# GpSimd makes the scaled and clamped scores of VectorE's exponential

## What is computed

```python
def wl_step(acc, wl):
    cpm, iw = wl                       # cos(phase_modulators) of 16 heads, one weight
    m = cpm[None, :, None, None]
    scores = jnp.einsum('bhqd,bhkd->bhqk', Q * m, K * m) * SCALE
    scores = scores * jnp.cos(KERR * scores * scores)
    attn = jax.nn.softmax(scores, axis=-1)
    out = jnp.einsum('bhqk,bhkd->bhqd', attn, V)
    return (acc + out * iw, None)
```

## Time and profile before

| | us |
|---|---|
| median of 3 runs (6973.81 to 6976.5) | 6975.69 |
| the profiled execution | 6975.18 |
| its span, first to last instruction | 6973.7 |
| ScalarE busy in the span | 6796.0 |
| TensorE busy in the span | 6097.9 |
| VectorE busy in the span | 6061.4 |
| GpSimd busy in the span | 148.7 |

### The profile page before, as it was taken

How to read it: one execution, slowest core, us unless ns; L and a number is a source line. 1 busy time by engine, 2 the same in 40 slices (tenths; PEclk the granted TensorE clock), 3 DMA queues, 4 the chain that set the end, 5 groups by cost and what they waited for, 6 DMA issues and landing times.

```text
span 6973.7 us, 125248 instructions
## 1 busy us (share of the span) xinstructions
PE 6097.9 (87%) x47364; PEld 2296.8 (33%) x47364; DVE 6061.4 (87%) x8039; ACT 6796.0 (97%) x1209; POOL 148.7 (2%) x244
## 2 busy tenths in 40 slices
PE   7888888888889888889888898888888888988888
PEld 3222222222333333333333333333333333333336
DVE  7998899899888888898888888888988888888884
ACT  6999999999999999999999999999999999999993
POOL 0000000000000000000000000000000000000000
PEclk8999999999999999999999999999999999999999
DMA  2000000000101001000010010010010100100100
GB/s 60 3 5 5 5 3 5 5 3 5 33 22 30 18 28 30 17 28 27 22 30 23 22 30 18 28 30 17 28 30 20 30 25 20 30 18 28 30 16 35
DMA packets 60481, 150.52 MB, mean 22 GB/s; under 512 B 11168, under 2 KB 27424, under 8 KB 59680
## 3 DMA queue, kind: packets, MB, share of 16 engines
q1 hardware_dynamic: 52960, 136.89, 6.3%
q0 software_dynamic: 2816, 3.68, 0.8%
q10 hardware_dynamic: 4160, 2.10, 0.1%
HBM read 132.14 MB, written 10.49 MB: 20 GB/s over the span
## 4 chain that ended last, share of the span: by engine, by line
ACT 48%; PE 35%; issue 13%; ACTq 4%; DVE 1%; DMA 0%; SPq 0%; DVEq 0%
ACT ring L593 46%; PE pv L705 23%; ACTq L590 3%; PE sc L753 3%; PE pv L711 3%; PE tr L721 2%; PE sc L765 2%; ACT tile_h L632 1%; PE sc L1337 1%; PE tr L1347 1%; PE sc L672 1%; PE sc L653 0%; ACT L632 0%; ACTq L591 0%; PE sc L290 0%
## 5 line engine op out<-in xcount | busy, mean ns | idle before, releaser
L593 ACT ACTIVATE ring<-scores 128x7168 f32<-128x7168 f32 (+1 forms) x1023 | 6581.5, 6529 | 7.3 <-PE pv L711 3.6
L705 PE MATMUL pv<-ring,vh 128*32 128x512 f32 x30400 | 3944.4, 627 | 821.8 <-ACT ring L593 812.8
L705 PEld LDWEIGHTS pv<-ring,vh 128*32 128x32 f32 x30400 | 992.8, 114 | 3422.5 <-issue 2081.5
L862 DVE SCALAR_TENSOR_TENSOR vprobs<-ring,vprobs 128x1024 f32<-128x1024 f32 x592 | 725.3, 1225 | 20.4
L861 DVE SCALAR_TENSOR_TENSOR ring<-ring 128x1024 f32<-128x1024 f32 x592 | 725.2, 1225 | 20.3
L860 DVE SCALAR_TENSOR_TENSOR vprobs<-ring,vprobs 128x1024 f32<-128x1024 f32 x592 | 721.2, 1218 | 7.1
L833 DVE COPY scores<-sc 128x1024 f32<-128x1024 f32 (+1 forms) x512 | 601.3, 1216 | 111.3 <-PE sc L672 111.3
L823 DVE TENSOR_REDUCE rowmax<-sc 128x1 f32<-128x1024 f32 x512 | 599.7, 1213 | 20.0 <-PE sc L653 12.8
L711 PE MATMUL pv<-vprobs,vlast 128*32 128x512 f32 x2368 | 613.0, 592 | 3.7 <-DVE vprobs L862 2.5
L703 PE MATMUL pv<-vpower,vlast 128*32 128x512 f32 x2368 | 613.7, 594 | 0.0
L850 DVE TENSOR_SCALAR vprobs<-scores,scales_log 128x1024 int32<-128x1024 f32 (+1 forms) x592 | 440.7, 744 | 43.9 <-DVE vprobs L862 25.2
(11 more groups left out here) (161 smaller groups left out, 2572.9 us busy)
## 6 DMA issues: line engine op xcount, KB each, us to landing
tile_w<-in_L_ffn_w SPq DMA_DIRECT2D x192, 512.0 KB, 3.9
qt<-q_scratch SPq DMA_DIRECT2D x256, 36.0 KB
kt_<-k_scratch SPq DMA_DIRECT2D x256, 36.0 KB
ring<-in_L_ffn_w SPq DMA_DIRECT2D x2, 2048.0 KB, 10.5
ring<-in_L_attn_x ACTq DMA_DIRECT2D x4, 512.0 KB, 7.2
q_scratch<-ring SPq DMA_DIRECT2D x4, 512.0 KB, 3.9
k_scratch<-ring SPq DMA_DIRECT2D x4, 512.0 KB, 4.9
v_scratch<-ring SPq DMA_DIRECT2D x4, 512.0 KB, 5.0
```

The source lines that it names most:

```text
L593: nc.scalar.activation(ring[:, i % SLOTS, 0:cols], scores[:, bass.ds(n % 2, 1), :, :].rearrange("p o k s -> p (o k s)")[:, 0:cols], ACT.Ex ...
L705: last = nc.tensor.matmul(sums, vh[:, buf, kt, window], ring[:, w % SLOTS, kt * S + qh * HALF:kt * S + (qh + 1) * HALF], start=(first and ...
L862: nc.vector.scalar_tensor_tensor(probs, vmant, EXP2_BETA, probs, ALU.add, ALU.mult).then_inc(vexp_step, 1)
```

## The change

GpSimd makes the scaled and clamped scores of every block (`make_bits`) into `vprobs`, and VectorE's `exponents` starts at the exponent and mantissa, behind a new semaphore `bits_made`. The factor is read from a small copy that GpSimd makes once per head (`copy_scale`), 16 numbers per partition. What VectorE waited for before L850 (all scores of the head, and the stream buffer read by TensorE) GpSimd now waits for. `head_bits` has the blocks 2 to 9 (or 8) of a head, with the fetch of the next head's values behind block 3, and then the blocks 0 and 1 of the next head. The store of an output tile follows the two heads of a pair.

```diff
-VSTEPS = 7
-POWER_STEP = 2
+VSTEPS = 6
+POWER_STEP = 1
...
+        def copy_scale(pool, n, odd):
+
+            nc.gpsimd.tensor_copy(head_scale[:, odd, :], scales_log2[:, :].rearrange("p (w h) -> p w h", h=H)[:, :, bass.ds(n % H, 1)].rearrange("p w o -> p (w o)")).then_inc(scale_copied, 1)
+
+        def make_bits(pool, n, waves, block, odd, first=False):
+
+            back = EARLY_BUFS if waves is EARLY_WAVES else LATE_BUFS
+            pool.wait_ge(scale_copied, n + 1)
+            pool.wait_ge(sc_free, USES * (n + 1))
+            if not first:
+                read = W * n + waves[block - back] if block >= back else W * (n - 1) + waves[block - back]
+                pool.wait_ge(slot_free, SLOTS + read + 1)
+            apart(pool)
+            w = waves[block]
+            nc.gpsimd.tensor_scalar(vprobs[:, stream(waves, block, odd), :].bitcast(I32), scores[:, odd, KT - 1, :],
+                                    head_scale[:, odd, w:w + 1], LOWEST, ALU.mult, ALU.max).then_inc(bits_made, 1)
+
+        def head_bits(pool, n, waves, odd, values=True, following=None):
+
+            for block in range(2, len(waves)):
+                make_bits(pool, n, waves, block, odd)
+                if block == 3 and values:
+                    copy_values(pool, n + 1, 1 - odd)
+            if following is not None:
+                copy_scale(pool, n + 1, 1 - odd)
+                make_bits(pool, n + 1, following, 0, 1 - odd)
+                make_bits(pool, n + 1, following, 1, 1 - odd)
...
             with pool.Fori(0, PAIRS - FIRST_PAIR - 1) as i:
-                store_tile(i)
-            store_tile(PAIRS - FIRST_PAIR - 1, True)
+                n = 2 * (i + FIRST_PAIR)
+                head_bits(pool, n, LATE_WAVES, 0, following=LATE_WAVES)
+                head_bits(pool, n + 1, LATE_WAVES, 1, following=LATE_WAVES)
+                store_tile(pool, i)
...
             base, at = share(m, waves, block), stream(waves, block, odd)
-            back = EARLY_BUFS if waves is EARLY_WAVES else LATE_BUFS
-            score = scores[:, bass.ds(m % 2, 1), KT - 1, :].rearrange("p o s -> p (o s)")
             bits = vprobs[:, at, :].bitcast(I32)
-            dve.wait_ge(sc_free, USES * (m + 1))
+            dve.wait_ge(bits_made, block_no(m, waves, block) + 1)
             if not first:
                 dve.wait_ge(vexp_step, base)
-                read = W * m + waves[block - back] if block >= back else W * (m - 1) + waves[block - back]
-                dve.wait_ge(slot_free, SLOTS + read + 1)
-            apart(dve)
-
             then = stepper(dve, vexp_step, base, [0])
-            then(nc.vector.tensor_scalar(bits, score, scales_log2[:, bass.ds(waves[block] * H + m % H, 1)], LOWEST,
-                                         ALU.mult, ALU.max))
             then(nc.vector.tensor_scalar(vpower[:, at, :].bitcast(I32), bits, EXPONENT, 0x40000000, ALU.bitwise_and, ALU.bitwise_xor))
```

More of the change, by code:

```diff
@@ L138, in build @@
         pm_sb = vprobs[:, 1, 0:W * H]
+        head_scale = sb("head_scale", [P, 2, W])
         rowmax = sb("rowmax", [P, KT])
@@ L487, in build @@
         vexp_step = sem("vexp_step")
+        scale_copied, bits_made = sem("scale_copied"), sem("bits_made")
         slot_free = sem("slot_free")
@@ L544, in sync_main, with block_no, stream @@
                 tile_loads(b * KT - 1, b < B - 1)
+        def block_no(n, waves, block):
+            return len(waves) * n + block + (EXTRA if waves is LATE_WAVES else 0)
+        def stream(waves, block, odd):
+            return block % EARLY_BUFS if waves is EARLY_WAVES else (block + odd * len(LATE_WAVES)) % LATE_BUFS
         def put_values(pool, n, buf):
@@ L558, in copy_values, with store_tile @@
             put_values(pool, n, buf)
+        def copy_scale(pool, n, odd):
[20 more added lines that the diff above has]
+                make_bits(pool, n + 1, following, 1, 1 - odd)
+        def store_tile(pool, i):
+            pool.wait_ge(tile_done, i + 1)
+            pool.dma_start(out_tiles[bass.ds(i, 1)].rearrange("o p e -> p (o e)"), tile_out[:, :]).then_inc(tile_stored, 16)
+            pool.wait_ge(tile_stored, 16 * (i + 1))
+            pool.sem_inc(tile_out_free, 1)
         def pool_main(pool):
@@ L564, in pool_main @@
             put_values(pool, 1, 1)
-            with pool.Fori(1, FIRST_PAIR) as i:
[L566 to L577, removed]
-            with pool.Fori(0, PAIRS - FIRST_PAIR - 1) as i:
-                store_tile(i)
-            store_tile(PAIRS - FIRST_PAIR - 1, True)
+            copy_scale(pool, 0, 0)
+            make_bits(pool, 0, EARLY_WAVES, 0, 0, first=True)
+            make_bits(pool, 0, EARLY_WAVES, 1, 0, first=True)
+            head_bits(pool, 0, EARLY_WAVES, 0, values=False, following=EARLY_WAVES)
+            head_bits(pool, 1, EARLY_WAVES, 1, following=EARLY_WAVES)
+            with pool.Fori(1, FIRST_PAIR) as i:
+                head_bits(pool, 2 * i, EARLY_WAVES, 0, following=EARLY_WAVES)
+                head_bits(pool, 2 * i + 1, EARLY_WAVES, 1, following=EARLY_WAVES)
+            with pool.Fori(0, PAIRS - FIRST_PAIR - 1) as i:
+                n = 2 * (i + FIRST_PAIR)
+                head_bits(pool, n, LATE_WAVES, 0, following=LATE_WAVES)
+                head_bits(pool, n + 1, LATE_WAVES, 1, following=LATE_WAVES)
+                store_tile(pool, i)
+            head_bits(pool, NH - 2, LATE_WAVES, 0, following=LATE_WAVES)
+            head_bits(pool, NH - 1, LATE_WAVES, 1, values=False)
+            store_tile(pool, PAIRS - FIRST_PAIR - 1)
         def scalar_main(act):
@@ L676, in share @@
         def share(n, waves, block):
-            return VSTEPS * (len(waves) * n + block + (EXTRA if waves is LATE_WAVES else 0))
-        def stream(waves, block, odd):
-            return block % EARLY_BUFS if waves is EARLY_WAVES else (block + odd * len(LATE_WAVES)) % LATE_BUFS
+            return VSTEPS * block_no(n, waves, block)
         def weigh_values(pe, n, buf, w, waves):
@@ L857, in polynomials @@
             base, probs = share(m, waves, block), vprobs[:, stream(waves, block, odd), :]
-            dve.wait_ge(vexp_step, base + 4)
-            then = stepper(dve, vexp_step, base, [4])
+            dve.wait_ge(vexp_step, base + 3)
+            then = stepper(dve, vexp_step, base, [3])
             then(nc.vector.scalar_tensor_tensor(probs, vmant, EXP2_GAMMA, probs, ALU.add, ALU.mult))
```

## The result

The changed kernel takes 7011.06 us in the median of 5 runs (7008.07 to 7015.92), the one before 6973.81 (6973.43 to 6976.5): **1.0053 times as long [1.0041, 1.0064], 37 us more**. I had predicted 6976, and 6998 as the upper end. The profiled execution took 7015.92 us, its span is 7014.3.

What follows compares the result with a forecast made beforehand. ScalarE was taken as the bound. The terms summed to 0 us against the profiled 6975.18; with at most 7.3 us to win and as much in new small waits, the forecast was 6976, own range 6968 to 6982, overall 6968 to 6998.

Steps and rivals of the forecast that it cites:

- What bounds the kernel: Whole kernel: ScalarE, busy 97% of the span, is the bound; a faster VectorE wins at most 7.3 us.
- ScalarE's idle time before the exponentials of 50 us or more: Sign of a wrong forecast, at ScalarE's exponentials, with TensorE waiting for VectorE's last result of a block in many wavelengths.
- GpSimd's operation over 2 us where VectorE does nothing beside it: Sign of a wrong forecast: GpSimd's new 128x1024 operation, forecast at 1.07 us, lasts over 2 us undisturbed.
- GpSimd's operation, put at 1.07 us with bounds of 0.74 and 2.8: Each of 592 new 128x1024 GpSimd operations: 0.23 us plus 1016 elements at 0.83 ns, a long write's rate.
- The block with the shortest notice: Wavelength 13 in early heads: GpSimd done some 1.2 us after starting, VectorE waits 0 to 0.2 us, covered by slack.
- What VectorE pays: SBUF meetings with GpSimd, every block: 0.65 us paid on average against 0.78 saved, so VectorE's load stays about the same.
- my rule of full payment: Assumed: a GpSimd operation meeting one of VectorE's six remaining instructions of a block costs VectorE its full length.
- VectorE becomes the bound: Rival, chance 0.08: from 1.77 us paid per early block, 2.22 per late, ScalarE waits; 7095 us at 2.3 us.
- VectorE's busy time stayed within 200 us of before: Sign of a right forecast: VectorE's total busy time changes by less than 200 us.
- The worst meeting in the tight place: Early heads: wavelength 14 late by 1.07 us against 1.5 of slack, 15 by 1.36 against 2.0; both hold.
- local lateness in the early heads: Rival, chance 0.08: an operation over 1.4 us frees wavelength 15's slot too late in 16 heads; 20 us, 6995.
- GpSimd's other work and the late heads: Value fetch and tile store stay covered, the store by 3 us; otherwise 3 us per pair meets the late lead of 5.8.

Runs made afterwards that it cites:

- the nine forms: Kernel before the change, with GpSimd alone running nine forms of one 128x1024 operation, three times each, at its start into unread scratch: 6979.03 us in one run.
- the run ahead: The change, but early heads' GpSimd results go into an idle tensor, waiting only for VectorE's reading two blocks back: 6976.88 us, 1.0004.

## Why the prediction was wrong

**What bounds the kernel: right.** ScalarE is the bound before and after, and its idle time before the exponentials, 7.3 to 44.8 us, is nearly the whole loss. "ScalarE's idle time before the exponentials of 50 us or more" as the mark of a wrong prediction was set a little too high, and "GpSimd's operation over 2 us where VectorE does nothing beside it" caught it.

**The term that failed: GpSimd's operation, put at 1.07 us with bounds of 0.74 and 2.8.** It takes 3.70 us alone. I took the rate of a write of 1024 elements as the nearest row. That row is right for what it is, and nearly for a copy (0.94 and 1.04 us), but it says nothing of arithmetic. The upper bound had three passes at that rate; by the differences between the nine forms the measured one is 1.04 us as for a copy, 1.8 more for the multiplication and 0.85 more for the clamp. The multiplications of 8 elements are too short to show a rate. The page GPSIMD Engine Reference of the Trainium skill (3.1) gives about 2.6 cycles per element, which it puts down to two inputs, and 1.03 cycles for bodies of at most two operations; at its 1.2 GHz these are estimates of 2.2 and 0.9 us for 1024 elements. The copy (1.04 us) is near the second; the multiplication (2.85 us) and the change's operation (3.70 us), with one tensor to read, take more than either.

**The block with the shortest notice: right place, wrong size.** I wrote of block 7 (wavelength 13) that GpSimd "is done some 1.2 us later" and VectorE "waits 0 to 0.2 us". VectorE stands 3.18 us there, and its next instruction comes 2.49 us later than before. The working follows the term above: 3.70 + 0.17 instead of 1.2. The run with VectorE keeping that block took back 32 of the 37 us, though it left a wait of 1.85 us at the next block, and the delay put in by itself gave the same time as the change, with hardly a meeting.

**What VectorE pays: near the mean by two errors.** I assumed that 61% of operations are paid in full, 0.61 x 1.07 = 0.65 us per block. It is 0.49, but of an operation of 3.7 us: 69% of the operations are met (411 of 592), and each of these costs 0.71 us on average. With the right length and my rule of full payment the sum would have been 0.61 x 3.7 = 2.3 us per block, which is what the rival "VectorE becomes the bound" asks for, 7095; its own condition, payment in full, is what the trace excludes. VectorE's busy time stayed within 200 us of before, as predicted.

**The worst meeting in the tight place.** For wavelength 14 I had 1.07 us of lateness against 1.5 of slack. It is 2.49 of waiting and 1.60 in two holds, less 1.32 saved: 2.77 us on VectorE and 2.15 on TensorE. VectorE may be 2.1 us late here before ScalarE waits, 0.58 to TensorE's use and 1.5 of slack. The holds without the wait would be 1.60 - 1.32 = 0.3 us, and the run ahead, with no wait and one hold, keeps all of its slack; the wait without the holds would be 2.49 - 1.32 = 1.2 us, though no run had that. In the change it takes both.

**The rival "local lateness in the early heads", 0.08, is what happened,** above its point of 1.4 us and in 16 heads. Its price of 20 us held for an operation of 2.0 us and counted only full holds; it lacked the wait for the result, and the second wait that a first one causes (1.57 us before wavelength 1 in every second head).

**GpSimd's other work and the late heads: right.** Three buffers are enough there: 430 operations on GpSimd cost 2 us or nothing, the fetch of values and the store of a tile stayed covered.

## What to carry to other kernels

A price from a row of another kind of operation (a write for a multiplication) is no price; where the nearest row does less work, the bound above must allow for several times it. When a step moves to an engine that is idle but slower, ask at the place with the shortest notice how long the step takes from the moment its buffer is free, and compare that with the slack there: idle share says nothing about it. If it doesn't fit, the same work may fit when it is started earlier into a buffer of its own (6976.88 instead of 7011.06 us here), and a slack that is only just kept is worth nearly as much as a large one (heads of 102.4 us with 0.2 us of it, 102.2 with 1.5).

## What the runs showed that I had not expected

- GpSimd needs 1.04 us for a copy of 128x1024, 2.85 for a multiplication with an integer result and at most 3.06 with a float one, 3.62 to 3.71 for multiplication and clamp, whatever the result's type.
- A GpSimd operation of 3.7 us holds VectorE up by about 0.8 us, once, in the instruction that follows its entry; VectorE runs at its normal rate beside the rest of it. One of 2.85 us holds it as long (0.80 us in the median of both traces), a copy of 1.04 us nearly so (0.72 us).
- Going from an operation of 3.70 to one of 2.85 us took away 29 of 37 us: the loss is a step at zero slack, and a first wait of ScalarE brings others behind it.
